# Two up-projection blocks behind the query, key and value projections, and six down-projection pieces behind the first turned keys

## The chip, the core and the metric

The kernel runs on one core of one Trainium2 chip. The time is that of the device, from start to end of one execution, in microseconds (us); of several executions the median is given. The engines of the core are called as in the profile: PE (TensorE, the matmuls) and PEld (its weight loads), DVE (VectorE), ACT (ScalarE), POOL (GpSimd), SP (SyncE, which issues most of the transfers). Each runs its own list of instructions in order and waits on semaphores that the others raise.

## What is computed

64 images are cut into patches of 16 x 16, two dense layers make a token of each, 32 text tokens are added to the 196 of an image, and one block of attention with a small MLP and one layer of eight experts follow. Cut to what matters:

```
def tok(x):                                      # 64 x 196 patches of 768
    return silu(patches(x) @ W1 + b1) @ W2 + b2  # 256 wide
def attn(x):                                     # 64 x 228 x 256, 16 heads of 16
    xn = rms_norm(x) * ln1_w
    q, k, v = xn @ Wq, xn @ Wk, xn @ Wv
    q, k = normalize(q), normalize(k)            # each head to length 1
    a = softmax(mask((q @ k.T + bias) * scale))
    y = (a @ v) @ Wo + x
    z = rms_norm(y) * ln2_w
    return relu(z @ W1) @ W2 + y                 # 256 -> 1024 -> 256
def ffn(x):                                      # each expert takes its 3648 best tokens
    scores = softmax(x @ Wr); G, idx = top_k(scores.T, 3648)
    return scatter_add(idx, G * (gelu(x[idx] @ W1 + b1) @ W2 + b2))
h = concat(tok(x), txt)
h = h + attn(layernorm(h))
h = h + ffn(layernorm(h))
```

## The kernel before

The kernel has two stages. The first, up to about 2650 us, goes over 32 pairs of images; a pair is 456 tokens, held as four tiles of 114. The second goes over the eight experts. The change lies in the first stage alone.

The first stage is a loop written as a pipeline by hand: in iteration i the engines finish the attention of pair i-1, run its MLP, and begin the attention of pair i. What PE does in an iteration, in its order (lines 848 to 864): second token layer of pair i, last turned outputs, output projection and transposes of pair i-1 (`pe_wo`, `pe_y2T`); the MLP's up projection `pe_w1` in eight blocks of six matmuls, 128 hidden columns each, blocks 0 to 2 ahead of the transposes of the normalised input (`pe_xsT`) and 3 to 7 behind them; the projections `pe_qkv` of pair i; and `pe_attention`. That begins with the down projection `pe_w2`, in 16 pieces of six matmuls: pieces 0 to 7 make the first half of the result (tiles 0 and 1), 8 to 15 the second. Then queries and keys are turned (`pe_qkT`, pair of heads by pair of heads), scores, exponentials and the products with v follow, head pair by head pair, with pieces 12 to 15 and the next pair's first token layer spread between them (`SLOTS`).

PSUM, where the matmuls write, is cut into banks: `G[0]` and `G[1]` go round between many blocks, in an order kept in the lists `ORDER` (a block waits until the block ahead of it in its bank's list was evacuated); `SC[0]` and `SC[1]`, of two banks each, hold the hidden blocks of the MLP (block m in `SC[m // 2 % 2][:, m % 2]`, so block 7 in the second bank of `SC[1]`) and later the scores; `Y` holds the attention's outputs. In the kernel before both halves of w2 go through `G[0]`, one behind the other.

What the other engines do for the MLP and the new queries and keys:

- Each product is made of float16 parts, a high and a low one. ACT makes the high part of a hidden block (`relu`, line 1101), then DVE the low one (`hid_low`, line 1405). Down-projection pieces read both.
- ACT copies the projections out (`queries_keys`, lines 1042 and 1047). DVE makes the norms (`qk_norm`): sums of squares (lines 1411, 1412), an inverse square root by Newton steps (lines 1419 to 1426), four scalings (line 1429). ACT casts each scaled tile (`high_parts`, line 1054), POOL casts it too (line 1810), and DVE makes the low parts (lines 1438, 1439). The turning on PE waits for both.
- `mlp_out` (line 1468) adds a half of the down projection to the residual, on DVE. In the kernel before, `mlp_out(part, j - 1, 0)` stands between the scalings and the low parts:

```
1427                for t in range(NT):
1428                    q = qkraw[:, t, :].rearrange("p (h d) -> p h d", d=HD)
1429                    dve.tensor_tensor(q, q, rn[:, t, :].unsqueeze(2).to_broadcast([T, 2 * H, HD]),
1430                                      ALU.mult).then_inc(qk_scaled, 1)
1432                if part.kind != "first":
1433                    mlp_out(part, j - 1, 0)
1434                for t in range(NT):
1435                    dve.wait_ge(qk_high, NT * j + (t + 1))
```

- `exps` on ACT: copies of turned keys and the exponentials (line 1063). ACT loads a table of its functions when the next function isn't in the one it holds.

Of the kernel before, what the change touches and what calls it, by code (L numbers as in the profile page):

```python
# [48 lines left out]
def early_fusion_kernel(nc, x, txt, tok_W1, tok_b1, tok_W2, tok_b2, ln1_w, Wq, Wk, Wv, rel_bias, scale, Wo,  # L49
# [52 lines left out]
    with ctx:  # L102
# [28 lines left out]
        def s1(name, shape, dt=F32):  # L131
            return sb(name, shape, dt, p1)
# [64 lines left out]
        w_sums = s1("w_sums", [128, 5])  # L197
        w_norms = s1("w_norms", [128, 6])
# [56 lines left out]
        def pb(name, shape):  # L255
# [31 lines left out]
        ones_ready, xs_high, y2_high = sem("ones_ready"), sem("xs_high"), sem("y2_high")  # L287
        hid_made, hid_high, hid_low_done = sem("hid_made"), sem("hid_high"), sem("hid_low_done")
# [34 lines left out]
            [("tok2", 0)] + BANKED["after"][0] + BANKED["front"][0] + BANKED["qkv"][0] + [("w2", 0), ("w2", 1)],  # L323
# [7 lines left out]
            "last": (BANKED["after"][0] + [("w2", 0), ("w2", 1)], BANKED["after"][1]),  # L331
# [130 lines left out]
        def pe_scores(part, j, g, first):  # L462
# [5 lines left out]
            if g == 1 and not first:  # L468
                pe.wait_ge(router_copied, j)
# [70 lines left out]

        W2_PIECES = [(b, 2 * b + t, m) for b in range(2) for t in range(2) for m in range(0, MC, 2)]

        def pe_w2(part, j, pieces):

            for n in pieces:
# [3 lines left out]
                if n % 8 == 0:  # L549
                    part.wait_free(pe, "w2", b)  # L550
                at = (t % 2) * D
                for m in (lo, lo + 1):
                    for i, (wp, hp) in enumerate(PARTS):
                        last = pe.matmul(part.g("w2", b)[0:T, at:at + D], hT[:, hp, m, t * T:(t + 1) * T], w2m[:, wp, m, :],  # L554
                                         start=m == 0 and i == 0, stop=m == MC - 1 and i == len(PARTS) - 1)
                if n % 8 == 7:
                    pe_block(part, ("w2", b), last)
# [25 lines left out]
        def pe_attention(part, j):  # L583
# [3 lines left out]
            for n in range(0, 12, 2):  # L587
                w2(n)
            pe_qkT(part, j, 0)
            pe_qkT(part, j, 1)  # L590
            pe_scores(part, j, 0, first)
# [235 lines left out]
        def _(eng):  # L827
# [20 lines left out]
            def iteration(part, i):  # L848
# [12 lines left out]
                for m in range(EARLY, MC):  # L861
                    pe_w1(part, i - 1, m)
                pe_qkv(part, i)
                pe_attention(part, i)
# [148 lines left out]
        def _(eng):  # L1013
# [128 lines left out]
            def iteration(part, i):  # L1142
# [6 lines left out]
                relu(i - 1, range(EARLY, MC))  # L1149
                queries_keys(part, i)  # L1150
                high_parts(i, range(NT))
                exps(part, i)
# [96 lines left out]
        def _(eng):  # L1249
# [42 lines left out]
            last.then_inc(qkv_folded, 1)  # L1292
            dve.memset(sum_ones[:, :], 1.0).then_inc(ones_ready, 1)
# [114 lines left out]
            def qk_norm(part, j):  # L1408
# [17 lines left out]
                step(dve.tensor_tensor(rn[:, :, 0:H], rn[:, :, 0:H], sc_q[:, :, :], ALU.mult))  # L1426
                for t in range(NT):
# [4 lines left out]
                if part.kind != "first":  # L1432
                    mlp_out(part, j - 1, 0)
# [494 lines left out]
```

## Time and profile before

| | us |
|---|---|
| median of 3 runs (4230.84 to 4241.97) | 4234.71 |
| the profiled execution | 4228.73 |
| its span, first to last instruction | 4226.9 |
| PE busy | 3665.6 (87%) |
| DVE busy | 2624.3 (62%) |
| ACT busy | 2081.8 (49%) |
| POOL busy | 1748.1 (41%) |

The profile is of one execution. Busy time is the time in which an engine executes an instruction; what is left is waiting, and the trace names for each wait the instruction that ended it. A share of busy time says which engine has the least room over the span; what one wait is worth is read in the timeline of the stretch where it lies. The granted clock of PE is given as a share of 2.4 GHz: 1.00, or 0.50 for 1.2 GHz.

### The profile page before, as it was taken

What the parts mean: (1) busy time and instruction counts of PE and PEld (TensorE: products, weight loads), DVE (VectorE), ACT (ScalarE), POOL (GpSimd) and SP (SyncE); (2) the same over time, 40 slices, a digit from 0 to 9 for tenths busy, and PEclk for the clock granted to TensorE, in tenths of its full rate; (3) what the DMA queues carried; (4) which work ended last, traced back from release to release, by engine and by line L of the source; (5) the groups of instructions that cost most, each with busy time, mean ns of one, the idle gap of its engine ahead of it and who ended that gap; (6) DMA issues with size and microseconds to landing.
All of it is one profiled execution on the core that took longest, in us unless ns stands there. A gap on an engine that the chain in (4) does not pass through costs nothing. (4 is left out here: it accounts for less than half of the span.)

```text
span 4226.9 us, 83054 instructions
## 1 busy us (share of the span) xinstructions
PE 3665.6 (87%) x28702; PEld 2376.2 (56%) x28702; DVE 2624.3 (62%) x5223; ACT 2081.8 (49%) x3393; POOL 1748.1 (41%) x1395
## 2 busy tenths in 40 slices
PE   2788888888889889889899898259999999999998
PEld 1466666666656656656666666135555555555554
DVE  3666766766666666666666665675555555555554
ACT  1544444444454454444444443326656555655655
POOL 1223333233233233233233231026666666666666
PEclk9899999999999999999999998569999999999999
DMA  7322312312322222222222210713333323323223
GB/s 137 43 37 43 50 37 42 50 37 42 50 40 43 47 41 46 41 45 46 38 47 48 34 30 10 211 36 46 65 64 46 65 45 66 63 44 66 46 46 46
DMA packets 297490, 219.83 MB, mean 52 GB/s; under 512 B 107846, under 2 KB 284680, under 8 KB 297208
## 3 DMA queue, kind: packets, MB, share of 16 engines
q1 hardware_dynamic: 188562, 155.40, 19.2%
q0 software_dynamic: 107264, 62.29, 9.5%
q8 instruction: 91, 1.49, 0.1%
q14 instruction: 77, 0.63, 0.0%
q10 hardware_dynamic: 1496, 0.01, 0.0%
HBM read 115.76 MB, written 62.74 MB: 42 GB/s over the span
## 5 line engine op out<-in xcount | busy, mean ns | idle before, releaser
L1690 DVE SCALAR_TENSOR_TENSOR hTs<-hTe,scales,hTs 128x456 f16<-128x456 f32 x514 | 322.7, 686 | 446.8 <-ACT hTs L1194 446.8
L1496 DVE TENSOR_TENSOR pr<-pr,bias_t 114x684 f32<-114x684 f32 x512 | 476.0, 955 | 175.6 <-ACT pr L1063 175.4
L1865 POOL DMA_INDIRECT out_dram<-contrib,idx_cur x256 | 537.5, 2100 | 109.4 <-issue 78.9
L554 PE MATMUL G<-w2m,hT 128*114 128x256 f16 x3072 | 424.8, 299 | 87.0 <-DVE stage L1468 87.0
L1063 ACT ACTIVATE pr<-SC 114x684 f32<-114x684 f32 x512 | 378.3, 745 | 240.7 <-PE SC L477 240.0
L937 PE MATMUL SC<-xgT,ws 128*128 128x456 f16 x2316 | 469.3, 357 | 0.0
L554 PEld LDWEIGHTS G<-w2m,hT 128*114 128x114 f16 x3072 | 385.3, 146 | 95.7 <-DVE stage L1468 94.9
L1858 POOL DMA_INDIRECT xg<-xn_rows,idx_cur x264 | 377.8, 1431 | 117.3 <-issue 61.2
L396 PE MATMUL G<-img,w1t 128*128 128x392 f32 x768 | 343.3, 538 | 74.5 <-DMA img<-turned 57.1
L937 PEld LDWEIGHTS SC<-xgT,ws 128*128 128x128 f16 x2316 | 227.4, 98 | 221.2 <-issue 3.7
L537 PE MATMUL SC<-yT,w1m 128*128 128x456 f16 x1536 | 318.0, 357 | 18.5 <-ACT yT L1095 11.2
L1791 POOL TENSOR_TENSOR rstd<-mv,ln_eps 114x4 f32<-114x4 f32 x32 | 22.9, 717 | 749.5 <-DVE mv L1354 749.5
L1194 ACT ACTIVATE hTs<-hTe,scales 128x456 f16<-128x456 f32 x514 | 330.5, 669 | 0.0
L1187 ACT ACTIVATE hTe<-SC,fb1c,unscales 128x456 f32<-128x456 f32 x386 | 280.7, 728 | 53.7 <-PE SC L937 52.2
L948 PE MATMUL Y<-hTs,ws 128*128 128x456 f16 x1536 | 306.3, 356 | 0.0
L948 PE MATMUL SC<-hTs,ws 128*128 128x456 f16 x1536 | 306.3, 356 | 0.0
L1810 POOL CAST qkp<-qkraw 114x256 f16<-114x256 f32 x128 | 86.0, 709 | 508.1 <-DVE qkraw L1429 508.1
L537 PEld LDWEIGHTS SC<-yT,w1m 128*128 128x128 f16 x1536 | 142.3, 98 | 175.8 <-ACT yT L1095 29.9
L1024 ACT COPY qkT<-G 128x912 f16<-128x912 f16 x128 | 117.4, 917 | 251.1 <-PE G L458 251.1
L475 PE MATMUL SC<-qkT 64*114 64x228 f16 x1024 | 160.1, 306 | 89.8 <-ACT qkT L1024 39.6
L1818 POOL COPY turned<-raw 96x1568 f32<-96x1568 f32 x64 | 197.9, 3092 | 90.6 <-DMA img<-turned 50.9
L1444 DVE COPY qkT<-G 128x912 f16<-128x912 f16 x128 | 81.0, 633 | 243.8 <-PE G L458 243.8
(269 smaller groups left out, 6957.9 us busy)
## 6 DMA issues: line engine op xcount, KB each, us to landing
raw<-in_x_dram SPq DMA_DIRECT2D x192, 196.0 KB, 6.2
img<-turned SPq DMA_DIRECT2D x384, 98.0 KB, 2.8
we<-in_L_ffn_W_dram SPq DMA_DIRECT2D x34, 1024.0 KB, 7.7
out_dram<-stage SPq DMA_DIRECT2D x32, 456.0 KB
xn_rows<-stage SPq DMA_DIRECT2D x32, 456.0 KB
xg<-xn_rows,idx_cur POOLq DMA_INDIRECT x264, 3.7
out_dram<-contrib,idx_cur POOLq DMA_INDIRECT x256, 5.5
bias_by_distance<-pr SPq DMA_DIRECT2D x1, 2429.6 KB, 30.1
```

The lines of the kernel that those rows point to most:

```text
L396: last = pe.matmul(part.g(*key)[:, 0:2 * NP_], w1t[:, k, m * 128:(m + 1) * 128], img[:, k, :, :].rearrange("p b n -> p (b n)"), start=k == ...
L537: last = pe.matmul(hid_bank(m), w1m[:, wp, c, m * 128:(m + 1) * 128], yh[:, yp, c, :], start=n == 0, stop=n == len(order) - 1)
L554: last = pe.matmul(part.g("w2", b)[0:T, at:at + D], hT[:, hp, m, t * T:(t + 1) * T], w2m[:, wp, m, :], start=m == 0 and i == 0, stop=m == ...
L937: last = pe.matmul(RING[bank2(key)][:, 0:W], ws1[eb][:, wp, c, m * 128:(m + 1) * 128], xgT[:, xp, c, :], start=c == 0 and i == 0, stop=c = ...
L948: last = pe.matmul(RING[bank2(key)][:, 0:W], ws2[eb][:, wp, m, c * 128:(c + 1) * 128], hTs[:, hp, m, :], start=m == 0 and i == 0, stop=m = ...
L1063: act.activation(pr[g % 4][:, :, :], SC[g % 2][0:T, :, 0:QW], ACT.Exp).then_inc(exp_done, 1)
L1187: act.activation(hTe[:, m, :], RING[bank2(key)][:, 0:W], ACT.Gelu, bias=bias[:, at:at + 1] if isinstance(at, int) else bias[:, bass.ds(at, ...
L1194: act.activation(hTs[:, 0, m, :], hTe[:, m, :], ACT.Identity, scale=scale_at(scales, 2, e)).then_inc(h_high, 1)
L1496: dve.tensor_tensor(pr[g % 4][:, :, :], pr[g % 4][:, :, :], bias_t[:, 2 * pair:2 * pair + 2, :], ALU.mult).then_inc(probs_done, 1)
L1690: dve.scalar_tensor_tensor(hTs[:, 1, m, :], hTe[:, m, :], scale_at(scales, 2, e), hTs[:, 0, m, :], ALU.mult, ALU.subtract).then_inc(h_spli ...
L1858: pool.indirect_dma_start(out=xg[k4][:, t, :], out_offset=None, in_=xd[:, :], in_offset=bass.IndirectOffsetOnAxis(ap=idx_cur[k4][:, t:t + ...
L1865: pool.indirect_dma_start(out=out_rows, out_offset=bass.IndirectOffsetOnAxis(ap=idx_cur[k4][:, t:t + 1], axis=0), in_=contrib[k][:, t, :], ...
```

## The change

Four things are done in every iteration of the loop but the first pair's.

1. PE runs w1 blocks 6 and 7 behind the projections and no longer ahead of them. ACT's relus 6 and 7 move behind its copies of the projections, and DVE's low parts 6 and 7 into `qk_norm`, between the Newton steps and the scalings.
2. The first half of w2 (pieces 0 to 7) is written to the second bank of `SC[1]`. Two new semaphores order this: `first_half_made` (PE to DVE) and `first_half_taken` (DVE to PE, waited for by scores 1, the first to write `SC[1]` again). Since the bank held hidden block 7, piece 0 waits for all eight low parts. The second half stays in `G[0]`, where it now follows v.
3. `mlp_out` of the first half moves behind the low parts of queries and keys, ahead of DVE's first copy of turned keys. Pieces 10 and 11 move behind the second turning, so that six pieces (10 to 15) follow the first turned keys.
4. ACT computes an exponential of one word (`warm`) behind its casts, so that the table is loaded there.

The core of the diff:

```
-            [("tok2", 0)] + BANKED["after"][0] + BANKED["front"][0] + BANKED["qkv"][0] + [("w2", 0), ("w2", 1)],
+            [("tok2", 0)] + BANKED["after"][0] + BANKED["front"][0] + BANKED["qkv"][0] + [("w2", 1)],
...
             if g == 1 and not first:
-                pe.wait_ge(router_copied, j)
+                pe.wait_ge(first_half_taken, j)
...
+        def w2_bank(part, b):
+            return SC[1][:, 1, :] if b == 0 else part.g("w2", 1)
...
-                if n % 8 == 0:
-                    part.wait_free(pe, "w2", b)
+                if n == 0:
+                    pe.wait_ge(hid_low_done, MC * j + MC)
+                if n == 8:
+                    part.wait_free(pe, "w2", 1)
...
-                if n % 8 == 7:
-                    pe_block(part, ("w2", b), last)
+                if n == 7:
+                    last.then_inc(first_half_made, 1)
+                if n == 15:
+                    pe_block(part, ("w2", 1), last)
...
-            for n in range(0, 12, 2):
+            for n in range(0, 10, 2):
                 w2(n)
             pe_qkT(part, j, 0)
             pe_qkT(part, j, 1)
+            w2(10)
             pe_scores(part, j, 0, first)
...
-                for m in range(EARLY, MC):
+                for m in range(EARLY, MC - 2):
                     pe_w1(part, i - 1, m)
                 pe_qkv(part, i)
+                for m in range(MC - 2, MC):
+                    pe_w1(part, i - 1, m)
                 pe_attention(part, i)
...
-                relu(i - 1, range(EARLY, MC))
+                relu(i - 1, range(EARLY, MC - 2))
                 queries_keys(part, i)
+                relu(i - 1, range(MC - 2, MC))
                 high_parts(i, range(NT))
+                act.activation(warm[:, 1:2], warm[:, 0:1], ACT.Exp).then_inc(exp_loaded, 1)
                 exps(part, i)
...
+                if part.kind != "first":
+                    hid_low(j - 1, range(MC - 2, MC))
                 for t in range(NT):
                     q = qkraw[:, t, :].rearrange("p (h d) -> p h d", d=HD)
...
-                if part.kind != "first":
-                    mlp_out(part, j - 1, 0)
                 for t in range(NT):
                     dve.wait_ge(qk_high, NT * j + (t + 1))
...
-                part.wait_filled(dve, "w2", b)
+                if b == 0:
+                    dve.wait_ge(first_half_made, j + 1)
+                else:
+                    part.wait_filled(dve, "w2", 1)
...
-                hid_low(i - 1, range(EARLY + 1, MC))
+                hid_low(i - 1, range(EARLY + 1, MC - 2))
                 qk_norm(part, i)
+                mlp_out(part, i - 1, 0)
                 masked_probs(part, i)
```

Three places show the new order. A row is an instruction by line (lines of the changed kernel are 2 to 18 higher), with the semaphores that it waits for.

PE of the kernel before, from the last v block (matmuls of `wqkv` with 256 columns) to piece 0 of w2 (matmuls of `w2m`):

```order
L443 MATMUL G<-wqkv,xsT 114x256 [waits evacuated1]
L443 MATMUL G<-wqkv,xsT 114x256 x11
L364 REGISTER_ALU [waits hid_low_done]
L554 MATMUL G<-w2m,hT 114x256 [waits evacuated0]
L554 MATMUL G<-w2m,hT 114x256 x5
```

PE of the changed kernel, the same place; matmuls of `w1m` are the up projection:

```order
L445 MATMUL G<-wqkv,xsT 114x256 [waits evacuated1]
L445 MATMUL G<-wqkv,xsT 114x256 x11
L530 REGISTER_ALU
L539 MATMUL SC<-yT,w1m 128x456 [waits hid_low_done]
L539 MATMUL SC<-yT,w1m 128x456 x5
L530 REGISTER_ALU
L539 MATMUL SC<-yT,w1m 128x456 [waits hid_low_done]
L539 MATMUL SC<-yT,w1m 128x456 x5
L555 REGISTER_ALU [waits hid_low_done]
L561 MATMUL SC<-w2m,hT 114x256 [waits hid_low_done]
L561 MATMUL SC<-w2m,hT 114x256 x5
```

Blocks 6 and 7 stand between v and piece 0, piece 0 writes `SC` instead of `G`, and waits for the low parts alone.

PE of the kernel before, from the second half of w2 (pieces 8 to 11) to scores 0 (`qkT` into `SC`); matmuls of `ident_h` are the turning:

```order
L554 MATMUL G<-w2m,hT 114x256 [waits evacuated0]
L554 MATMUL G<-w2m,hT 114x256 x23
L364 REGISTER_ALU [waits qk_copied,qk_normed]
L458 MATMUL G<-ident_h,qkp 128x114 [waits evacuated1]
L458 MATMUL G<-ident_h,qkp 128x114 x7
L364 REGISTER_ALU
L458 MATMUL G<-ident_h,qkp 128x114 [waits evacuated1]
L458 MATMUL G<-ident_h,qkp 128x114 x7
L467 ISA [waits evacuated1]
L475 MATMUL SC<-qkT 114x228 [waits exp_done]
```

PE of the changed kernel, the same place:

```order
L561 MATMUL G<-w2m,hT 114x256 [waits evacuated0]
L561 MATMUL G<-w2m,hT 114x256 x11
L366 REGISTER_ALU [waits qk_copied,qk_normed]
L460 MATMUL G<-ident_h,qkp 128x114 [waits evacuated1]
L460 MATMUL G<-ident_h,qkp 128x114 x7
L366 REGISTER_ALU
L460 MATMUL G<-ident_h,qkp 128x114 [waits evacuated1]
L460 MATMUL G<-ident_h,qkp 128x114 x7
L561 MATMUL G<-w2m,hT 114x256 x12
L469 ISA [waits evacuated1]
L477 MATMUL SC<-qkT 114x228 [waits exp_done]
```

Twelve of the 24 matmuls now follow the second turning. The wait on `evacuated0` ahead of them is for `mlp_out` of the first half before, and for ACT's copy of v in the changed kernel.

DVE of the kernel before, from the last Newton step to the first low parts of queries and keys:

```order
L1426 TENSOR_TENSOR rn<-rn,sc_q 114x4x16 [waits dve_step]
L1429 TENSOR_TENSOR qkraw<-qkraw,rn 114x512 [waits dve_step]
L1429 TENSOR_TENSOR qkraw<-qkraw,rn 114x512 x3
L1468 SCALAR_TENSOR_TENSOR stage<-G,r,stage 114x256 [waits filled0,hy_done,r2_done]
L1468 SCALAR_TENSOR_TENSOR stage<-G,r,stage 114x256
L1438 TENSOR_TENSOR qkp<-qkraw,qkp 114x16x16 [waits qk_high]
```

DVE of the changed kernel, the same place:

```order
L1441 TENSOR_TENSOR rn<-rn,sc_q 114x4x16 [waits dve_step]
L1420 SCALAR_TENSOR_TENSOR hT<-SC,hT 128x456 [waits hid_high,dve_step]
L1420 SCALAR_TENSOR_TENSOR hT<-SC,hT 128x456 [waits hid_high]
L1446 TENSOR_TENSOR qkraw<-qkraw,rn 114x512 x4
L1453 TENSOR_TENSOR qkp<-qkraw,qkp 114x16x16 [waits qk_high]
```

The two hidden low parts (into `hT`) stand ahead of the scalings, and `mlp_out` (into `stage`) has left the place.

## Rows read from the trace of the kernel before

**Rows 1.** Page, first part: busy us, share of the span, instructions.

```profile
PE 3665.6 (87%) x28702; PEld 2376.2 (56%) x28702; DVE 2624.3 (62%) x5223; ACT 2081.8 (49%) x3393; POOL 1748.1 (41%) x1395
```

**Rows 2.** Waits of PE, 200 to 2600 us: us in total, times, longest.

```profile
PE G L554 <- DVE stage L1468: 85.9, 31, 2.8
PE SC L475 <- ACT qkT L1024: 38.4, 57, 1.1
```

**Rows 3.** Timeline of PE in one iteration: start us, us, instruction, count [idle before].

```profile
1053.32 5.94 PE L537 MATMUL SC<-yT,w1m 128*128 128x456 f16 x30
1059.10 5.34 PE L436 MATMUL G<-wqkv,xsT 128*114 128x512 f16 x24
...
1066.90 5.40 PE L554 MATMUL G<-w2m,hT 128*114 128x256 f16 x48
1075.08 4.50 PE L554 MATMUL G<-w2m,hT 128*114 128x256 f16 x24 [2.78 <-DVE stage L1468]
1079.41 0.56 PE L458 MATMUL G<-ident_h,qkp 114*128 114x114 f16 x8
...
1082.29 0.31 PE L475 MATMUL SC<-qkT 64*114 64x228 f16 x2 [0.44 <-DVE qkT L1444]
...
1084.94 0.31 PE L475 MATMUL SC<-qkT 64*114 64x228 f16 x2 [1.13 <-ACT qkT L1024]
```

**Rows 4.** Timeline of DVE, the same iteration.

```profile
1053.93 1.16 DVE L1393 TENSOR_TENSOR xsT<-G,xsT 128x456 f16<-128x456 f32 x2
...
1057.16 1.16 DVE L1405 SCALAR_TENSOR_TENSOR hT<-SC,hT 128x456 f16<-128x456 f32 x2
...
1061.32 0.69 DVE L1411 TENSOR_TENSOR sqb<-qkraw 114x512 f32<-114x512 f32 x1 [0.74 <-ACT qkraw L1042]
...
1071.35 2.89 DVE L1429 TENSOR_TENSOR qkraw<-qkraw,rn 114x512 f32<-114x512 f32 x4
1074.17 0.86 DVE L1468 SCALAR_TENSOR_TENSOR stage<-G,r,stage 114x256 f32<-114x256 f32 x2
...
1078.04 0.21 DVE L1439 COPY qkp<-qkp 114x256 f16<-114x256 f16 x1
```

**Rows 5.** Windows: stretch, us, busy of each engine, PEclk, DMA share, GB/s.

```profile
1072.30:1075.08 2.78, 0.01 (x1) 0.00 (x0) 2.78 (x6) 2.23 (x4) 2.55 (x4) 1.00 0.00 0
1075.50:1078.90 3.40, 3.40 (x19) 3.40 (x17) 2.75 (x11) 0.00 (x0) 0.00 (x0) 0.50 0.00 0
249.82:328.28 78.46, 69.38 (x632) 48.34 (x633) 53.38 (x112) 37.31 (x63) 25.65 (x25) 0.98 0.25 43
2369.45:2447.91 78.46, 69.38 (x632) 48.36 (x633) 53.36 (x112) 37.32 (x63) 25.65 (x25) 0.98 0.26 43
```

**Rows 6.** Timeline of ACT, the iteration of rows 3.

```profile
1060.60 0.69 ACT L1042 ACTIVATE qkraw<-G,w_unscale 114x512 f32<-114x512 f32 x1 [0.69 <-PE G L436]
...
1074.28 0.62 ACT L1054 CAST qkp<-qkraw 114x512 f16<-114x512 f32 x1 [0.18 <-DVE qkraw L1429]
1080.02 0.92 ACT L1024 COPY qkT<-G 128x912 f16<-128x912 f16 x1 [5.12 <-PE G L458]
1081.97 1.28 ACT L1063 ACT_TABLE_LOAD   x1 [1.03 <-PE SC L477]
```

**Rows 7.** Timeline of POOL, the same iteration.

```profile
1072.18 2.67 POOL L1810 CAST qkp<-qkraw 114x256 f16<-114x256 f32 x4 [16.21 <-DVE qkraw L1429]
```

**Rows 8.** Timeline of PE and windows at two borders of experts, second stage.

```profile
3513.78 4.74 PE L937 MATMUL G<-xgT,ws 128*128 128x456 f16 x12 [3.39 <-issue]
...
3864.70 3.90 PE L937 MATMUL G<-xgT,ws 128*128 128x456 f16 x12 [3.19 <-issue]
...
3512.60:3513.80 1.20, 0.02 (x1) 0.03 (x2) 1.20 (x4) 0.00 (x0) 0.19 (x1) 0.51 0.02 7
3513.80:3519.40 5.60, 5.60 (x15) 2.22 (x16) 3.98 (x5) 1.41 (x3) 4.93 (x3) 0.50 0.17 35
...
3864.20:3864.70 0.50, 0.00 (x1) 0.01 (x1) 0.50 (x3) 0.00 (x0) 0.14 (x1) 0.50 0.00 0
3864.70:3867.60 2.90, 2.90 (x8) 1.18 (x9) 2.22 (x3) 0.21 (x1) 1.66 (x3) 0.50 0.10 19
```

More of the change, by code:

```diff
@@ L197, in early_fusion_kernel @@
         w_sums = s1("w_sums", [128, 5])
+        warm = s1("warm", [1, 2])
         w_norms = s1("w_norms", [128, 6])
@@ L287, in early_fusion_kernel @@
         ones_ready, xs_high, y2_high = sem("ones_ready"), sem("xs_high"), sem("y2_high")
+        first_half_made, first_half_taken, exp_loaded = sem("first_half_made"), sem("first_half_taken"), sem("exp_loaded")
         hid_made, hid_high, hid_low_done = sem("hid_made"), sem("hid_high"), sem("hid_low_done")
@@ L330, in early_fusion_kernel @@
             "final": (body[0] + BANKED["turn"], body[1]),
-            "last": (BANKED["after"][0] + [("w2", 0), ("w2", 1)], BANKED["after"][1]),
+            "last": (BANKED["after"][0] + [("w2", 1)], BANKED["after"][1]),
         }
@@ L553, in pe_w2 @@
                     for i, (wp, hp) in enumerate(PARTS):
-                        last = pe.matmul(part.g("w2", b)[0:T, at:at + D], hT[:, hp, m, t * T:(t + 1) * T], w2m[:, wp, m, :],
+                        last = pe.matmul(w2_bank(part, b)[0:T, at:at + D], hT[:, hp, m, t * T:(t + 1) * T], w2m[:, wp, m, :],
                                          start=m == 0 and i == 0, stop=m == MC - 1 and i == len(PARTS) - 1)
-                if n % 8 == 7:
-                    pe_block(part, ("w2", b), last)
+                if n == 7:
+                    last.then_inc(first_half_made, 1)
+                if n == 15:
+                    pe_block(part, ("w2", 1), last)
         SLOTS = {n: [] for n in range(2 * NG)}
@@ L1292, in _ @@
             last.then_inc(qkv_folded, 1)
+            dve.memset(warm[:, :], 0.0)
             dve.memset(sum_ones[:, :], 1.0).then_inc(ones_ready, 1)
@@ L1464, in mlp_out @@
                 dve.wait_ge(hy_done, 2 * (j + 1))
-                part.wait_filled(dve, "w2", b)
+                if b == 0:
+                    dve.wait_ge(first_half_made, j + 1)
+                else:
+                    part.wait_filled(dve, "w2", 1)
                 for half in range(2):
                     t = 2 * b + half
-                    last = dve.scalar_tensor_tensor(hy[:, t, :], part.g("w2", b)[0:T, half * D:(half + 1) * D],
+                    last = dve.scalar_tensor_tensor(hy[:, t, :], w2_bank(part, b)[0:T, half * D:(half + 1) * D],
                                                     r2[:, t:t + 1], hy[:, t, :], ALU.mult, ALU.add)
-                last.then_inc(evacuated[part.bank("w2", b)], 1)
+                last.then_inc(first_half_taken if b == 0 else evacuated[part.bank("w2", 1)], 1)
             def mlp_stats(part):
```

## Prediction

> **What bounds the kernel now.** I read four views in this order. The page gives the shares: TensorE (PE) is busy for 87% of the span [rows 1], so it sets the pace, and what can be won on it are its waits and the stretches at its lower clock. The waits of PE over the 31 loop iterations of the first stage (about 200 to 2600 us; the expert stage behind them is not touched) name one that stands out: 31 waits, 85.9 us in sum, before line 554, released by VectorE (DVE) line 1468; next come 57 waits, 38.4 us, for ScalarE's (ACT) copies of turned keys [rows 2]. The timeline of one iteration shows where: PE runs 48 matmuls of the down projection w2 (pieces 0 to 7) until 1072.30, stands until 1075.08, runs 24 more (pieces 8 to 11), and turns the first queries and keys at 1079.41 [rows 3]. DVE's timeline says why: the wait ends with mlp_out(0) at 1075.03, which stands in DVE's order behind the four key scalings, though pieces 0 to 7 had long been there [rows 4]. The windows show a second cost: the granted clock is 1.00 (2.4 GHz) during the wait and 0.50 (1.2 GHz) from 1075.5 to 1078.9 [rows 5], so the 24 matmuls take 1079.41 - 1075.08 = 4.33 us, where at the pace of the 48 ahead of them (5.40 / 48 = 0.1125 us each) they would take 2.70. The fall costs 1.63 us, the wait 2.78.
>
> **The change, part by part,** in the times of that iteration.
>
> *Two of eight w1 blocks go behind the projections.* One block is 6 of the 30 matmuls that start at 1053.32 and hand over at 1059.10: 5.78 / 5 = 1.156 us [rows 3]. The projections so start 2.31 us earlier, at 1056.79. Nothing holds them there: the low parts of xs, which they wait for, end at 1055.09, and DVE's hidden parts 4 and 5, which stand ahead of the sums of squares, end at 1058.32 [rows 4]. ACT copies the first tile at 1060.60 - 2.31 = 1058.29 [rows 6], where its two late relus no longer stand ahead of it. DVE starts the sums at 1061.32 - 2.31 = 1059.01 and, being the slower of the two, keeps its 10.03 us from there to the scalings [rows 4]: it comes to 1069.04. PE's own work is only swapped in order, so w1 still ends at 1066.90.
>
> *The new wait.* The late hidden parts 6 and 7 now stand on DVE between that chain and the scalings: two cost 1.16 us (the pair at 1057.16 [rows 4]). They end at 1069.04 + 1.16 = 1070.20. Piece 0 now waits for all eight (its bank in SC[1] held hidden block 7), so PE stands from about 1067.0 to 1070.25: 3.2 us. The old wait of 2.78 at piece 8 is gone, because piece 8 writes another bank. Queued behind the waiting PE are ten pieces and the turning; the new wait is longer than the old, and the trade is good only because it comes before 60 matmuls that DVE's scalings and low parts can hide behind.
>
> *What DVE does meanwhile.* Scalings 1070.2 to 1073.1 (2.89), low parts without mlp_out ahead of them: from 1075.03 to 1078.25 they take 3.2, so to 1076.3 [rows 4]. ACT's and POOL's casts follow the scalings as before (ACT's last from 1074.28, POOL's four in 2.67 us [rows 6, 7]), and both move 1.15 us earlier with them: neither is last. mlp_out(0) now follows the low parts and takes its 0.86 while PE runs and turns; scores 1, the first that waits for it, come over 3 us after the turning begins, so it costs nothing. Without that cover it would cost 0.86.
>
> *PE up to the turning.* Ten pieces (60 matmuls) from 1070.25 take 6.75 us at the fast pace: 1077.0, later than the 1076.3 of DVE, so PE sets the start. With a fall that costs the same 1.63 it is 1078.6. Before it was 1079.41: a gain of 2.4 or 0.8.
>
> *Behind the turning.* Pieces 10 and 11 (12 matmuls, 1.35 us) stand between the second turning and scores 0. They cover the 0.44 us wait of scores 1, and delay scores 0 by 1.35. ACT's table load of 1.28 us, today between scores 0 and the first exponential [rows 6], moves behind the casts, where ACT stands idle for 5 us; what it hides under is that idle time, else 1.28 come back. So scores 0 come 1.3 later and the exponential needs 1.3 less: scores 2, before which PE stands 1.13 us today, came 1084.94 - 1079.41 = 5.53 us behind the turning [rows 3] and come 5.6 behind it: the exponential starts at 3.8, ends at 4.5, ACT's next copy ends near 5.5. I charge 0.07. Left are 2.3 (no fall) and 0.7 (a fall as today).
>
> *The clock.* The trace has no wait at this place of 3.2 us, so its price lies between these ends, and beyond on one side. The nearest rows are two waits of PE at borders of experts. Behind the one of 3.19 us the clock is at 0.50 for the last 0.5 us of the wait and for 2.9 us of work; behind the one of 3.39 us for the last 1.2 us of the wait and 5.6 us of work [rows 8]. By the first, the low clock takes 2.9 us of work instead of 3.4, which gives back 0.5 x 1.63 / 3.4 = 0.24. I take that row, as its wait is the same to 0.01 us: 0.7 + 0.24 = about 0.95 us in an iteration.
>
> The Trainium skill (TensorE: Matmul & The Clock Gate, in the section on HAM oscillation) speaks against this change: waits between bursts of matmuls make the engine fall back and pay the way up again each time round. By that rule alone, with today's price in every iteration, the sum would be 31 x 0.7 = 22 us. The trace agrees in kind: the 31 waits of 2.8 us come with a clock of 0.50 behind them.
>
> *Sum.* 31 x 0.95 = 29.5 us. The profiled execution took 4228.73 us (span 4226.9); the gain in it would lead to 4199. The median of the runs is 6 us higher, 4234.71, and the same gain leads to 4205, which I forecast. Once, behind the loop, the 16 pieces run again with one wait replaced by another of about its size: at most one iteration's worth, left out.
>
> **Rivals.** *The clock holds in half of the iterations or more.* In the three rows the clock falls 0.4 us behind the end of a wait, or 0.5 or 1.2 us before it [rows 5, 8]: the moment isn't tied to the wait's start, and today's loop repeats so evenly that it always meets the same moment. With another period it may split the wait so that neither side of it shows enough standing. Half of the iterations at 2.3 and half at 0.95 give 31 x 1.6 = 50 us, 4185; all at 2.3 give 71, 4163. Against it: an early and a late iteration have the same mean clock of 0.98 [rows 5], one fall of 3.4 us in 78.5 each, so today's wait brings it every time. The Trainium skill (same page, What's actually happening) says that the gate looks at the activity in its own running time, not from a kernel's start, which would let the same wait fall differently from one iteration to the next; no run here shows that yet.
>
> *The low clock lasts twice as long, and the change loses.* The 3.39 us wait had 5.6 us of low work behind it [rows 8]. At 1.63 / 3.4 = 0.48 us lost per low us that is 2.7 where no fall is worth 2.3: 0.4 us lost in an iteration, 31 x 0.4 = 12, or 4247. With 6.8 us all on work it is 3.26, a loss of 0.95 and 4264. It decides above 2.3 / 0.48 = 4.8 us of low work in an iteration. For it: the wait becomes longer, near the size of that row. Against: the nearer row shows 2.9.
>
> *Given back in part.* Low work between 3.9 and 4.8 us, or a table load or copy that isn't hidden, leaves under 0.4 us in an iteration: within 12.7 us of before.
>
> *The projections don't start earlier.* If the sums stayed at 1061.32, the new wait would be 5.5 us and the turning 1.5 us later than today: 31 x 1.5 = 47, 4281. The 1.7 us of room between xs and the projections speaks against it [rows 3, 4].
>
> **How the numbers follow.** A measurement of this kernel tells about 0.3%, 12.7 us, from no change. Forecast (about 4190 to 4220) 0.52; clock holds 0.21; given back, 4222 to 4246, 0.17; low clock longer 0.07; projections not earlier 0.03. Faster: 0.52 + 0.21 = 0.73, same 0.17, slower 0.10. The range from 4165 to 4240 leaves out the last two, the upper end of the given back and the lowest end of the clock that holds, near 0.17 together.
>
> **What would show it.** In the profile after: the waits of PE for mlp_out (1468 of before) gone from the top; 31 new waits of about 3.2 us before the first w2 matmul, released by the hidden parts of DVE; first turning some 0.8 to 2.4 us earlier against the start of the iteration; no table load between scores 0 and the first exponential; PE's idle time in an iteration nearly the same. Wrong would be: a new wait far over 3.5 us (then the start of the projections is the step that failed), or a low clock of another length behind it (then the clock's price).

## The result, and the profile after

| | before | after |
|---|---|---|
| median, us | 4232.77 | 4184.65 |
| lowest to highest of 4 runs | 4227.16 to 4241.97 | 4182.2 to 4188.7 |
| the profiled execution, us | 4228.73 | 4182.2 |
| its span, us | 4226.9 | 4180.4 |

The ratio is 0.9881, with a 95% interval of 0.9865 to 0.9897: 1.2% faster. It lies in the range, but 20 us below the forecast of 4205 and outside the 4190 to 4220 that had the best chance; it meets the 4185 of the rival by which the clock holds in half of the iterations.

The page of the kernel after, first part (busy us, share of the span, instructions), answers to [rows 1]. PE has the same instructions and is busy 42 us less:

```profile
PE 3624.0 (87%) x28702; PEld 2335.8 (56%) x28702; DVE 2633.1 (63%) x5224; ACT 2085.8 (50%) x3424; POOL 1761.9 (42%) x1395
```

The waits of PE from 200 to 2560 us (us in total, times, longest) answer to [rows 2]. The wait for `mlp_out` is gone from the top, and 31 waits for a hidden low part of DVE stand in its place, longer than it was. The turning's wait (line 460) isn't new, it only has another neighbour:

```profile
PE SC L561 <- DVE hT L1420: 101.9, 31, 3.3
PE G L460 <- ACT qkT L1036: 31.3, 31, 1.0
PE SC L477 <- ACT qkT L1036: 25.9, 62, 0.5
```

PE's timeline of one iteration, which begins at 1404.76, answers to [rows 3] (start us, us, instruction, count, idle before). The last two rows are from the iteration that begins at 1480.76:

```profile
1426.66 5.34 PE L438 MATMUL G<-wqkv,xsT 128*114 128x512 f16 x24
...
1440.23 5.45 PE L561 MATMUL SC<-w2m,hT 128*114 128x256 f16 x48 [3.30 <-DVE hT L1420]
1445.52 1.47 PE L561 MATMUL G<-w2m,hT 128*114 128x256 f16 x12
1446.83 0.56 PE L460 MATMUL G<-ident_h,qkp 114*128 114x114 f16 x8
...
1448.82 1.48 PE L561 MATMUL G<-w2m,hT 128*114 128x256 f16 x12
...
1452.39 0.31 PE L477 MATMUL SC<-qkT 64*114 64x228 f16 x2 [0.49 <-ACT qkT L1036]
...
1516.23 7.12 PE L561 MATMUL SC<-w2m,hT 128*114 128x256 f16 x48 [3.30 <-DVE hT L1420]
...
1524.50 0.56 PE L460 MATMUL G<-ident_h,qkp 114*128 114x114 f16 x8
```

Both iterations have the same wait of 3.30 us, but the 60 matmuls behind it take 1446.83 - 1440.23 = 6.60 us in the first and 1524.50 - 1516.23 = 8.27 in the second. The windows (stretch, us, busy of PE, PEld, DVE, ACT, POOL, granted clock, DMA share, GB/s) say why; they are the two iterations, the stretches behind the wait, and at last 28 iterations together, after and before, beside [rows 5]:

```profile
1404.76:1480.76 76.00, 67.50 (x632) 46.54 (x633) 53.61 (x112) 37.45 (x64) 25.82 (x25) 1.00 0.25 45
1480.76:1558.47 77.71, 69.17 (x632) 48.20 (x633) 53.70 (x112) 37.50 (x64) 25.82 (x25) 0.98 0.26 44
1440.23:1446.83 6.60, 6.59 (x60) 6.59 (x61) 6.60 (x17) 3.94 (x6) 2.86 (x4) 1.00 0.00 0
...
1516.23:1517.15 0.92, 0.92 (x8) 0.92 (x9) 0.92 (x2) 0.34 (x1) 0.23 (x1) 1.00 0.03 2
1517.15:1520.56 3.41, 3.41 (x19) 3.41 (x18) 3.41 (x8) 3.03 (x5) 2.62 (x4) 0.50 0.00 0
1520.56:1524.50 3.94, 3.94 (x38) 3.93 (x38) 2.92 (x10) 0.58 (x2) 0.00 (x0) 1.00 0.00 0
248.68:2405.58 2156.90, 1918.87 (x17697) 1329.78 (x17697) 1502.79 (x3136) 1048.63 (x1765) 718.74 (x700) 0.99 0.26 44
...
249.82:2447.91 2198.09, 1949.62 (x17696) 1359.56 (x17697) 1494.58 (x3136) 1044.21 (x1737) 718.23 (x700) 0.97 0.25 43
```

In the first the granted clock stays at 1.00 (2.4 GHz); in the second it is 0.50 (1.2 GHz) for 3.41 us, through which 19 matmuls run. That makes 8.27 - 6.60 = 1.67 us. An iteration has taken 2156.90 / 28 = 77.03 us. Before, the same 28 took 2198.09, 78.50 each. The 1.47 us between them, 28 times, are 41 of the 46.5 us that the span lost; 249.82 - 248.68 = 1.1 lie ahead of these iterations, the other 4.2 behind them. PE's idle time in an iteration hardly changed, as the prediction said: (2198.09 - 1949.62) / 28 = 8.87 us before and (2156.90 - 1918.87) / 28 = 8.50 after. So of the 1.47 only 0.37 is less waiting; 1.10 is the same matmuls in less time.

### The profile page after: what moved, and what is told of

It reads as the page before. It is cut to its first block and busy times, and to the rows that moved or that the text cites. A ratio compares the mean times of both kernels' runs of the same rounds, so it can differ in the third digit from the quotient of the medians.

```text
span 4180.4 us, 83027 instructions
## 1 busy us (share of the span) xinstructions
PE 3624.0 (87%) x28702; PEld 2335.8 (56%) x28702; DVE 2633.1 (63%) x5224; ACT 2085.8 (50%) x3424; POOL 1761.9 (42%) x1395
## 5 line engine op out<-in xcount | busy, mean ns | idle before, releaser
L1877 POOL DMA_INDIRECT xg<-xn_rows,idx_cur x264 | 394.9, 1496 | 117.2 <-issue 61.2
L561 PE MATMUL SC<-w2m,hT 128*114 128x256 f16 x1536 | 201.6, 299 | 103.3 <-DVE hT L1420 103.3
L561 PEld LDWEIGHTS SC<-w2m,hT 128*114 128x114 f16 x1536 | 193.8, 146 | 117.6 <-DVE hT L1420 117.6
L960 PEld LDWEIGHTS SC<-hTs,ws 128*128 128x128 f16 x1536 | 150.1, 98 | 133.6
L960 PEld LDWEIGHTS Y<-hTs,ws 128*128 128x128 f16 x1536 | 147.3, 99 | 133.6
```

The costliest lines, as they stand in the source:

```text
L561: last = pe.matmul(w2_bank(part, b)[0:T, at:at + D], hT[:, hp, m, t * T:(t + 1) * T], w2m[:, wp, m, :], start=m == 0 and i == 0, stop=m == ...
L960: last = pe.matmul(RING[bank2(key)][:, 0:W], ws2[eb][:, wp, m, c * 128:(c + 1) * 128], hTs[:, hp, m, :], start=m == 0 and i == 0, stop=m = ...
L1877: pool.indirect_dma_start(out=xg[k4][:, t, :], out_offset=None, in_=xd[:, :], in_offset=bass.IndirectOffsetOnAxis(ap=idx_cur[k4][:, t:t + ...
```

## The experiments

Counted over the same 28 iterations of each profiled execution, with the granted clock of the trace: a fall is a stretch at 0.50, "without" the iterations that have none. Ratios are to the kernel before, run again beside each group (medians 4231.70 to 4236.66), with 95% intervals.

| kernel | median us | ratio | iteration, mean | without a fall: how many, us | low clock in an iteration, us |
|---|---|---|---|---|---|
| before | 4232.77 | 1 | 78.50 | 0 | 4.02 |
| b_busy | 4225.57 | 0.9984 (0.9973 to 0.9995) | 78.46 | 6, 77.39 | 3.90 |
| b_warm | 4228.14 | 0.9995 (0.9981 to 1.0009) | 78.37 | 1, 76.73 | 5.97 |
| after | 4184.65 | 0.9881 (0.9865 to 0.9897) | 77.03 | 12, 76.00 | 2.19 |
| a_busy | 4156.04 | 0.9813 (0.9795 to 0.9832) | 76.10 | 26, 75.98 | 0.24 |
| a_w1_ahead | 4259.64 | 1.0073 (1.0051 to 1.0095) | 79.22 | 0 | 7.44 |
| a_ahead | 4227.99 | 0.9989 (0.9979 to 0.9999) | 78.49 | 0 | 5.00 |
| a_cold | 4261.12 | 1.0056 (1.0038 to 1.0074) | 79.46 | 0 | 4.75 |
| a_low_sooner | 4173.67 | 0.9858 (0.9837 to 0.9879) | 76.63 | 5, 75.93 | 2.80 |
| a_between | 4191.32 | 0.9895 (0.9877 to 0.9913) | 77.14 | 3, 75.38 | 4.02 |
| a_between_busy | 4134.58 | 0.9767 (0.9747 to 0.9786) | 75.38 | 28, 75.38 | 0 |
| a_both | 4140.30 | 0.9772 (0.9755 to 0.9790) | 75.60 | 20, 75.29 | 0.98 |
| a_both_busy | 4133.70 | 0.9767 (0.9748 to 0.9787) | 75.35 | 27, 75.29 | 0.12 |

The theory: the order gives an iteration about 0.7 us with a fall in it as before, and the rest of the gain is that some iterations have none. The rival: the gain is the wait itself that went, and the clock changes little.

### The wait filled with work, in both kernels

To take the fall away without touching the order, PE is given matmuls whose results nobody reads, in the time in which it would stand. They stand in the new wait in `a_busy`, 15 of them, and in the old one, between pieces 7 and 8, 13, in `b_busy` (which waits for `MC * j + MC` there):

```
+        def pe_standing_work(j, n):
+            pe.wait_ge(hid_low_done, MC * j + (MC - 2))
+            for k in range(n):
+                pe.matmul(SC[0][:, 0, 0:W], w1m[:, 0, 0, 0:128], yh[:, 0, 0, :], start=True, stop=True)
 a_busy:
+                pe_standing_work(i - 1, 15)
                 pe_attention(part, i)
 b_busy:
             for n in range(0, 8, 2):
                 w2(n)
+            if not first:
+                pe_standing_work(j - 1, 13)
             for n in range(8, 12, 2):
                 w2(n)
```

> The changed kernel, with 15 such matmuls (about 2.9 us) in the new wait of 3.3 us. If the iterations of the changed kernel differ only by the fall of the clock (76.0 without one, 77.7 with one), all of them now take 76.0, and 17 falls of about 1.7 us are saved: 29 us, about 4155. Rival: the pattern of 76.0 and 77.7 comes from something else that goes in pairs (image loads, buffers): the pattern stays, 4184.

Measured: 4156.04 us, as expected. PE's timeline and the window of 28 iterations of a_busy:

```profile
283.69 5.45 PE L567 MATMUL SC<-w2m,hT 128*114 128x256 f16 x48 [0.40 <-DVE hT L1427]
...
248.23:2378.93 2130.70, 1974.13 (x18117) 1345.90 (x18117) 1501.29 (x3136) 1048.53 (x1765) 718.81 (x700) 1.00 0.26 45
```

The wait shows 0.40 us, w2 starts no earlier, and yet 26 of the 28 iterations take 75.98. So the order after makes an iteration of 76.0, and the 1.03 us by which the mean of after is longer are the clock's alone; the rival of something else that goes in pairs falls.

> The kernel before, with 13 matmuls whose result nobody reads (w1 by y2, into the first bank of SC[0], about 2.5 us) put where TensorE stands for 2.78 us ahead of piece 8; nothing else is moved. If the fall of the clock behind that wait costs 1.63 us in an iteration, as worked out, this alone gives 31 x 1.63 = 50 us: about 4182, with a granted clock of 1.00 in the loop and the iteration at 76.8 instead of 78.45. Rival: the clock falls for another reason, or the 4.33 us of the 24 matmuls are bound by their weights: no change, 4233.

Measured: 4225.57 us, far from what was expected, and near the rival's 4233. PE's timeline of b_busy (line 545 holds the unread matmuls), and windows of an iteration without a fall and one with a fall:

```profile
364.57 2.67 PE L545 MATMUL SC<-yT,w1m 128*128 128x456 f16 x13
367.51 2.83 PE L560 MATMUL G<-w2m,hT 128*114 128x256 f16 x24 [0.27 <-DVE stage L1478]
370.80 0.57 PE L458 MATMUL G<-ident_h,qkp 114*128 114x114 f16 x8 [0.47 <-DVE qkp L1449]
...
327.32:404.70 77.38, 70.38 (x646) 47.90 (x646) 53.38 (x112) 37.20 (x63) 25.62 (x25) 1.00 0.26 44
404.70:483.37 78.67, 71.82 (x646) 49.05 (x646) 53.38 (x112) 37.36 (x63) 25.62 (x25) 0.98 0.25 43
```

Of the rival's two reasons the weights are out: the 24 matmuls now take 2.83 us. Two things took the gain. First, the turning then waits 0.47 us for DVE's low parts, which `mlp_out` stands ahead of; in the kernel before, the slow matmuls had hidden that. And the clock still falls: 22 of 28 iterations have one, now in the stretch of turnings and scores, where PE has short waits. So without a fall the old order takes 77.4 and the new 76.0, and with one fall 78.4 and 77.7. The order is worth 0.7 to 1.4 us, by whether the clock falls.

### The parts undone, one at a time

`a_w1_ahead` puts w1 blocks 6 and 7, their relus and their low parts back ahead of the projections, and keeps the rest:

```
-                for m in range(EARLY, MC - 2):
+                for m in range(EARLY, MC):
                     pe_w1(part, i - 1, m)
                 pe_qkv(part, i)
-                for m in range(MC - 2, MC):
-                    pe_w1(part, i - 1, m)
... (the relus on ACT and the low parts on DVE likewise)
```

> The changed kernel with w1 blocks 6 and 7, their relus and low parts where they were before; the rest of the change stays. Pieces 0 to 9 then run on without a wait behind v, to about 1073.5 in the times of before, but scalings and low parts come late: 1074.24 + 3.2 = 1077.4, so TensorE stands for about 4 us ahead of the first turning instead. If the move of the blocks is worth only what separates 1077.4 from 1076.9, plus the clock that now falls on sparser work, this costs 0.5 to 1.0 us in an iteration without a fall and less where one was: 4180 to 4200. Rival: the move is the change's heart, and without it the time goes back to 4220 or more.

Measured: 4259.64 us, above the kernel before. Window and PE's timeline of one iteration of a_w1_ahead, and its 28 iterations:

```profile
411.37:490.55 79.18, 69.60 (x633) 48.44 (x633) 53.80 (x112) 37.48 (x64) 25.81 (x25) 0.96 0.25 43
...
454.47 0.94 PE L460 MATMUL G<-ident_h,qkp 114*128 114x114 f16 x8 [4.38 <-DVE qkp L1449]
...
457.15 2.77 PE L561 MATMUL G<-w2m,hT 128*114 128x256 f16 x12
...
462.18 0.31 PE L477 MATMUL SC<-qkT 64*114 64x228 f16 x2 [0.50 <-ACT qkT L1034]
...
252.16:2470.29 2218.13, 1953.31 (x17697) 1361.31 (x17697) 1505.91 (x3136) 1050.64 (x1765) 722.81 (x700) 0.95 0.25 43
```

The wait now stands ahead of the turning, 4.38 us, and the clock falls there in all 28 iterations: in the one shown eight turning matmuls take 0.94 us (0.56 in after), the twelve of w2 2.77 (1.48). The turning starts 454.47 - 411.37 = 43.10 us into the iteration, 1.03 later than in after without a fall: that is the order's part, at the upper end of the 0.5 to 1.0 expected. Scores 2 come 462.18 - 454.47 = 7.71 us behind the turning; in after 5.56. So the fall costs 2.15 here, where the clock is low for 6.83 us, 5.75 of them behind the wait. The mean iteration is 79.22 - 77.03 = 2.19 us longer than in after, 1.03 of it by the order and 1.16 by the clock. The time is that of the rival, 4220 or more, but not for its reason alone: what was expected priced the clock too low.

`a_ahead` puts pieces 10 and 11 back ahead of the first turning:

```
-            for n in range(0, 10, 2):
+            for n in range(0, 12, 2):
                 w2(n)
             pe_qkT(part, j, 0)
             pe_qkT(part, j, 1)
-            w2(10)
```

> The changed kernel with pieces 10 and 11 ahead of the first turning again. The turning comes 1.3 us later, scores 2 then 4.75 us behind it instead of 5.56: 0.5 us lost in an iteration, 16 us, about 4200, give or take 15 for another pattern of falls. Rival: the two pieces only change places with waits and nothing is lost: 4184.

Measured: 4227.99 us, above what was expected. PE's timeline of an iteration of a_ahead that begins at 410.17:

```profile
453.54 0.56 PE L460 MATMUL G<-ident_h,qkp 114*128 114x114 f16 x8
...
458.36 0.44 PE L477 MATMUL SC<-qkT 64*114 64x228 f16 x2
```

The order's part came out: the turning is 1.30 us later (43.37 us into the iteration), scores 2 come 4.82 behind it (5.56 in after), a loss of 0.56. The rest is the clock: no iteration is without a fall, and their 5.00 us at the low clock are more than the 2.19 of after. The first two have one fall at the wait and take 78.27 and 78.22, some 0.55 more than the 77.67 that are usual in after with one fall; the others alternate between about 77.5, with a fall behind the turnings, and about 79.5, with one of 6.83 us that begins 0.8 ahead of the wait's end.

`a_cold` leaves out the exponential of one word:

```
-                act.activation(warm[:, 1:2], warm[:, 0:1], ACT.Exp).then_inc(exp_loaded, 1)
```

> The changed kernel without the exponential of one word, so that the table is loaded ahead of the first real one again. If the load is hidden now and was on the path before, it costs its 1.28 us in each iteration, 31 x 1.28 = 40 us, and the wait of TensorE for ACT's next copy grows from 0.49 to about 1.8 us, where the clock may fall as well: 4225 to 4260. Rival: the load only fills a wait: 4184.

Measured: 4261.12 us, 1 us above the upper end. ACT's timeline of a_cold, and PE's:

```profile
460.08 1.28 ACT L1075 ACT_TABLE_LOAD   x1 [2.35 <-PE SC L479]
...
463.05 0.31 PE L477 MATMUL SC<-qkT 64*114 64x228 f16 x2 [1.77 <-ACT qkT L1036]
```

The table is loaded between scores 0 and the first exponential, and scores 2 wait 1.77 us in place of 0.49: all of the 1.28 us comes back. The mean iteration is 79.46 - 77.03 = 2.43 us longer than in after; the 1.15 beside the load are of the clock, which falls 38 times in the 28 iterations. (Its usual iteration with one fall takes 78.93; less the 1.67 of a fall that is 77.26, longer by the load than the 76.00 of after.) `b_warm` does the opposite, it adds that one exponential to the kernel before.

> The kernel before with the exponential of one word behind ACT's casts, and nothing else of the change. The 1.13 us wait ahead of scores 2 falls to about 0.45: 0.7 us in an iteration, 31 x 0.7 = 21 us, about 4212, if the clock falls once in each iteration as before; down to 4190 if the shorter iteration lets some pass without a fall. Rival: the table load is on the path only together with the other parts: 4233.

Measured: 4228.14 us, no change. Windows of b_warm, a usual iteration and the 28:

```profile
409.18:487.72 78.54, 70.77 (x633) 49.55 (x633) 53.38 (x112) 37.69 (x64) 25.62 (x25) 0.96 0.25 43
252.84:2447.24 2194.40, 1972.12 (x17696) 1378.85 (x17697) 1494.75 (x3136) 1054.77 (x1765) 717.42 (x700) 0.96 0.25 43
```

The clock in an iteration is 0.96 where it was 0.98: there are 49 falls in 28 iterations, two in most, at the 2.78 us wait and behind the turnings. The one iteration without a fall took 76.73, and the five with a single one 77.60 to 77.77, some 0.7 less than the 78.41 of before: the gain that was expected is there, and a second fall takes it back in the other 22. So each of the three parts undone costs nearly the whole gain or more, and the one part tried alone brings nothing: their times don't add up, since each also changes where and how often the clock falls. The new bank of the first half and the place of `mlp_out` were not undone by themselves.

### Further along the same way

`a_low_sooner` puts the late low parts ahead of the last of three Newton steps, so that the new wait ends sooner:

```
-                for _ in range(3):
+                for turn in range(3):
+                    if turn == 2 and part.kind != "first":
+                        hid_low(j - 1, range(MC - 2, MC))
                     step(dve.tensor_tensor(a_, r_, r_, ALU.mult))
...
-                if part.kind != "first":
-                    hid_low(j - 1, range(MC - 2, MC))
```

> The changed kernel with hidden low parts 6 and 7 ahead of the last of the three Newton steps instead of behind them. Piece 0 then starts about 1.3 us sooner and the wait ahead of it falls from 3.3 to 2.0 us; the scalings stay where they are, so VectorE's low parts (about 0.5 us sooner than the turning is today) become the bound of the first turning. If a shorter wait keeps the clock up, 0.5 us in an iteration and 17 falls of 1.7 us are saved: 31 x 0.5 + 29 = 44, about 4140. If the clock falls as often as now, 4169.

Measured: 4173.67 us, near the second of the two. PE's timeline of a_low_sooner:

```profile
358.58 5.45 PE L561 MATMUL SC<-w2m,hT 128*114 128x256 f16 x48 [2.05 <-DVE hT L1420]
...
366.32 0.57 PE L460 MATMUL G<-ident_h,qkp 114*128 114x114 f16 x8 [0.98 <-DVE qkp L1454]
```

The wait is down from 3.30 to 2.05, but 0.98 of it comes back at the turning: DVE has the same work up to its last low part, and now ends after PE. An iteration without a fall is 75.93, 0.07 less than in after. 23 of 28 have a fall, 15 at this wait and 8 behind the first turning. The 15 cost only about 0.5 us each (76.4 in place of 75.9), since the slow matmuls take the place of the 0.98 us wait at the turning; the 8 cost 1.5.

`a_between` moves pieces 10 and 11 from behind the second turning to between the two, where PE stood 1.01 us for ACT:

```
             pe_qkT(part, j, 0)
-            pe_qkT(part, j, 1)
             w2(10)
+            pe_qkT(part, j, 1)
```

> The changed kernel with pieces 10 and 11 between the first and the second turning, where TensorE stands 1.01 us for ACT's copy, instead of behind the second. Scores 0 then come 2.25 us behind the first turning instead of 3.39, scores 2 about 0.9 us sooner: 31 x 0.9 = 28 us, about 4156 with the clock's falls as now; from 4130 to 4185 by how they meet the new period. Rival: the second turning, 0.2 us later, holds VectorE's copy and the exponentials: 4184.

Measured: 4191.32 us, slower than after and above the range. Windows of a_between, an iteration without a fall and the 28:

```profile
400.98:476.37 75.39, 67.54 (x633) 46.66 (x633) 53.58 (x112) 37.57 (x64) 25.80 (x25) 1.00 0.27 45
250.22:2410.24 2160.02, 1940.59 (x17696) 1355.67 (x17697) 1502.95 (x3136) 1051.51 (x1765) 722.73 (x700) 0.97 0.26 44
```

The order does what was meant, 75.38 in place of 76.00, though it gives 0.62 and not 0.9. But only 3 of 28 iterations are without a fall, where after had 12. `a_between_busy` has the same order with 15 unread matmuls in the wait, as in a_busy:

> The run with two pieces between the turnings, and 15 matmuls for nobody in the wait of 3.3 us. That run has iterations of 75.4 without a fall, but nearly all of its later ones took 76.7 to 78.3. If its disappointing 4191 is the falls alone, all iterations now take 75.4: 4156 - 31 x 0.6 = 4137 (from the changed kernel with the same 15 matmuls). Rival: the second turning, now behind the pieces, costs as well: 4156.

Measured: 4134.58 us, as expected. All 28 iterations take 75.38:

```profile
251.00:2361.61 2110.61, 1971.95 (x18117) 1347.07 (x18117) 1500.76 (x3136) 1052.32 (x1765) 722.83 (x700) 1.00 0.26 45
```

Of the 4191.32 - 4134.58 = 57 us between the two, 2160.02 - 2110.61 = 49 lie in these 28 iterations, and they are the clock's. It settles the matter: a better order ran slower because of its falls (4.02 us at the low clock in an iteration, 2.19 in after), and not because of anything in the order. The rival of the second turning falls too.

`a_both` joins a_low_sooner and a_between, with no unread work:

> The two edits together, low parts sooner and two pieces between the turnings: gains of 0.5 and 0.9 us in an iteration and no falls: 31 x 1.4 + 29 = 72, about 4112. If the gains of the two are one and the same wait, 4140.

Measured: 4140.30 us (4138.69 to 4141.12), the number of the second, but not its reason. Without a fall an iteration takes 75.29, 0.71 less than in after, and the two edits alone had 0.07 and 0.62: the gains add up, each was only smaller than expected. Nor are the falls gone: 8 of 28 iterations have one, four at the wait of 2.05 us and four among the scores. That this adds up to 4140 is luck. Why 20 iterations have none, where the edits alone left 5 and 3, is not shown. It beats both kernels, the one after by 1.1%. `a_both_busy` fills what is left of its wait with 9 unread matmuls:

> The run with both edits, and 9 matmuls for nobody (about 1.7 us) in its wait of 2.05 us. Its iterations take 75.3 without a fall, and about one in three had one, worth 0.5 or 1.6 us, most of them behind the turnings and not at this wait. If the falls all hang on the wait, 4140 - 12 = 4128; if those behind the turnings stay, 4133 to 4140.

Measured: 4133.70 us, 27 of 28 iterations at 75.29, one with a fall. By the ratios that is 0.05% from a_both, within the intervals: hardly anything is left of the clock's price, and what remains is the order.

## Why the prediction was right, point by point

**Two w1 blocks behind the projections.** Right. DVE starts the sums of squares 1428.88 - 1404.76 = 24.12 us into the iteration; before it was 1061.32 - 1034.89 = 26.43 [rows 3, 4], with 1034.89 the start of that iteration. That is 2.31 earlier, as worked out, so the rival of projections that don't start earlier falls. DVE's timeline of after:

```profile
1428.88 0.69 DVE L1426 TENSOR_TENSOR sqb<-qkraw 114x512 f32<-114x512 f32 x1 [0.68 <-ACT qkraw L1054]
...
1439.01 1.17 DVE L1420 SCALAR_TENSOR_TENSOR hT<-SC,hT 128x456 f16<-128x456 f32 x2
1440.10 2.89 DVE L1446 TENSOR_TENSOR qkraw<-qkraw,rn 114x512 f32<-114x512 f32 x4
1442.90 1.15 DVE L1453 TENSOR_TENSOR qkp<-qkraw,qkp 114x256 f16<-114x256 f32 x2
1443.98 0.21 DVE L1454 COPY qkp<-qkp 114x256 f16<-114x256 f16 x1
1444.11 0.75 DVE L1453 TENSOR_TENSOR qkp<-qkraw,qkp 114x256 f16<-114x256 f32 x2
...
1446.39 0.21 DVE L1454 COPY qkp<-qkp 114x256 f16<-114x256 f16 x1
1446.53 0.86 DVE L1486 SCALAR_TENSOR_TENSOR stage<-SC,r,stage 114x256 f32<-114x256 f32 x2
```

**The new wait.** 3.30 us for 3.2.

**What DVE does meanwhile.** Right in its order, and off in one size: the low parts took 1446.60 - 1442.90 = 3.70 us, not 3.2, mostly as the first pair took 1.15 in place of the 0.74 of before:

```profile
1074.95 0.74 DVE L1438 TENSOR_TENSOR qkp<-qkraw,qkp 114x256 f16<-114x256 f32 x2
```

DVE was done 0.23 us ahead of the turning in the iteration without a fall, not 0.7: the cover was thinner than worked out. It is just this that a_low_sooner ran into, where DVE ended last. `mlp_out` is hidden behind it, as foreseen.

**PE up to the turning.** 6.60 without a fall for 6.75, and a fall costs 1.67 for 1.63. Against the start of the iteration the turning is at 42.07 or 43.74; before at 1079.41 - 1034.89 = 44.52. The gain of 2.45 or 0.78 answers to 2.4 or 0.8.

**Behind the turning.** Scores 2 come 1452.39 - 1446.83 = 5.56 us behind it, for 5.6, with a wait of 0.49 where [rows 3] had 1.13. The table load is hidden, as ACT's timeline of after shows; without that cover (a_cold) it cost the whole 1.28:

```profile
1443.65 1.28 ACT L1165 ACT_TABLE_LOAD   x1
1444.95 0.20 ACT L1165 ACTIVATE warm<-warm 1x1 f32<-1x1 f32 x1
```

**The clock.** This is the term that was mis-sized. The forecast took 0.24 us off a fall by the expert border of 3.19 us [rows 8] and put that in every iteration: 0.95. Measured is another split. A fall costs 1.67, no less than before, for it begins 0.92 us behind the end of the wait and lies wholly on work; 12 of the 14 falls at the wait begin so, 0.64 to 1.21 us behind its end. But a fall comes in 16 of 28 iterations: 14 at the wait, 2 among the scores. An iteration with one is mostly 78.41 - 77.67 = 0.74 shorter than before, as the 0.7 worked out; one without is 78.41 - 76.00 = 2.41 shorter, for 2.3. The 12 without gain 1.67 more than the others, 0.72 as a mean, and 0.74 and 0.72 are nearly the whole 1.47. (What is rarer cancels: two falls in after last 6.83 us, and five iterations of before have a second one.)

The price for low time on work held: in a_between eight falls begin 0.59 us ahead of the wait's end, 2.82 of their 3.41 us lie on work, and they cost 76.74 - 75.38 = 1.36, again 0.48 us for each us. So a fall that lies partly in the wait does cost less; wrong was to put one in every iteration of after. The nearness of the wait's length to a row was no ground for taking that row's price: the same 3.30 us wait costs 0 in one iteration and 1.67 in the next.

**The rivals.** That the clock holds in half of the iterations or more had 0.21 and nearly happened, in 12 of 28. That its 4185 was met to 1 us is in part luck: it put the other half at 0.95, where iterations with one fall gained 0.74 and the two with a long fall lost 0.4, and 4.2 us of the gain lie behind these iterations. The first half of its reason held: the fall isn't tied to the wait's start, since the same wait has one in half of the iterations. That it is the new period that no longer meets the same moment each time fits this, but no run shows it. The reading of before was a little too even there as well: its 28 iterations have 33 falls, not 28, and reach from 78.40 to 78.84 us. The Trainium skill (TensorE: Matmul & The Clock Gate, What's actually happening) says that the gate looks at the activity in its own running time; the trace agrees in so far as neighbours with the same wait take 76.00 and 77.71 us. By the section on HAM oscillation of the Trainium skill (same page) the gain would have been 22 us, with the price paid each time round; measured were 48, and the price was paid in 16 of 28. In a_w1_ahead, where the wait stands ahead of the turnings, it was paid in all 28. That the low clock lasts twice as long, the rival on the other side, did not happen here in the mean (2.19 us in an iteration, 4.02 before). It did happen twice: two of the falls at the wait last 6.83 us, and these iterations take 78.81 and 78.83, longer than the 78.41 of before. a_w1_ahead, with a longer wait (4.38 us), had 7.44 us in the mean and was slower than before.

**What stays open.** Why the falls come as they do. Before, b_busy, a_ahead and b_warm are four orders with means of 78.37 to 78.50, though an iteration without a fall takes 77.4 in b_busy and 76.7 in b_warm: the falls gave back nearly all that b_busy and b_warm gain without them. That is measured; that the loop settles there by some rule is not shown. Nor was it told beforehand which order has few falls: the expectations that missed (b_busy, a_w1_ahead, a_ahead, b_warm and a_between) all missed there, b_busy and a_w1_ahead only in part.

## What to carry to other kernels

What a fall of the clock costs depends on how much of its low time lies on work, and on what stands behind that: 1.67 us for 3.41 ahead of 60 matmuls, 1.36 where 0.59 of it lay in the wait, about 0.5 where PE waited again soon after (a_low_sooner), 2.15 for 6.83 ahead of an exchange with ACT (a_w1_ahead). That a wait has fewer falls in one place than in another is not shown: a_w1_ahead moved its wait and made it longer as well, and a_ahead had a fall in every iteration with its 3.30 us wait ahead of 72 matmuls. When a loop has waits of a few us, price the clock as none, half and all of the iterations, and judge an edit by its iterations without a fall beside its mean: a better order can run slower until the wait is filled (4191 against 4135). Filling the wait with unread matmuls tells the two apart in one run, and filling it with the kernel's own pieces (a_both) gets nearly the same without them.

## What the runs showed of the hardware

Work that nobody reads can make a kernel faster: in a_busy PE was busy for 1974.13 us over 28 iterations, in after for 1918.87, and those iterations took 2130.70 in place of 2156.90.

Of the 224 low-part instructions of DVE on 114x256 most take about 410 ns in either kernel, but in after the longest takes 614, and in before 413. The long ones are the first pair of each iteration, beside which POOL's casts run. In after the casts end at 1443.77, while the first pair of low parts runs from 1442.90; before they ended at 1074.85, ahead of the low parts [rows 4, 7]. POOL's timeline of after, and the group of these DVE instructions, after and before (least, median and longest ns):

```profile
1440.91 2.86 POOL L1829 CAST qkp<-qkraw 114x256 f16<-114x256 f32 x4 [15.09 <-DVE qkraw L1446]
...
L1453 DVE TENSOR_TENSOR qkp<-qkraw,qkp x224: 409/412/614, 286.8 to 2370.9; 114x256 f16<-114x256 f32 x112
...
L1438 DVE TENSOR_TENSOR qkp<-qkraw,qkp x224: 406/410/413, 289.9 to 2412.3; 114x256 f16<-114x256 f32 x112
```

The casts took 2.86 us, where [rows 7] has 2.67. The Trainium skill (GPSIMD Engine Reference, Specifications) says that the two engines share interfaces to SBUF, with contention for DVE instructions that read two inputs from there, as these do; the trace agrees in kind, with 0.4 us for the pair and 0.2 for the casts. It does not prove it: ACT's casts run beside the same pair, and no run took either away.
